# Two recurrent scans on one core: loops written out step by step, and four identity products in half-width tiles

## What is computed

```python
def _L1_conv_ref(feature, conv_w, conv_b, prelu_a):
    Wc = conv_w[:, :, 0, 4]
    def step(prev, x_i):
        y = jnp.einsum('oc,nch->noh', Wc, prev) + conv_b[None, :, None]
        y = jnp.where(y >= 0, y, prelu_a * y)
        cur = y + x_i
        return (cur, cur)
    x = jnp.moveaxis(feature, 3, 0)
    _, fwd_rest = jax.lax.scan(step, x[0], x[1:])
    fl = jnp.concatenate([x[0:1], fwd_rest], axis=0)
    _, bwd_rest = jax.lax.scan(step, fl[-1], fl[:-1], reverse=True)
...
x = x + _L0_conv_ref(_gn(x), ...)
x = x + _L1_conv_ref(_gn(x), L1_conv_conv_w, L1_conv_conv_b, L1_conv_prelu_a)
x = x + _L2_conv_ref(_gn(x), ...)
x = x + _L3_conv_ref(_gn(x), L3_conv_W, L3_conv_b)
```

## Time and profile before

| | |
|---|---|
| median of three runs | 253.15 us (253.0 to 253.29) |
| the profiled execution | 252.99 us |
| its span, first to last instruction | 251.2 us |
| busy: matmul, vector, scalar, POOL | 246.5, 168.1, 97.7, 87.7 us |
| scan 1, first to last matmul | 68.6 to 128.5 us of the span |
| scan 3, first to last matmul | 192.4 to 248.7 us |
| granted TensorE clock | full speed all through |

### The profile page before, as it was taken

One profiled execution on the slowest core, in us unless ns is written; L12 is line 12 of the kernel. 1 busy time (PEld: TensorE's weight loads), 2 busy tenths in 40 slices (PEclk: granted clock), 3 DMA queues, 4 the chain that ended last, 5 costly groups with the idle time before them and its releaser, 6 DMA issues.

```text
span 251.2 us, 11069 instructions
## 1 busy us (share of the span) xinstructions
PE 246.5 (98%) x4492; PEld 218.9 (87%) x4492; DVE 168.1 (67%) x655; ACT 97.7 (39%) x231; POOL 87.7 (35%) x138
## 2 busy tenths in 40 slices
PE   8999999999999999999999999999999999999995
PEld 2778787888699999999997887788887999999995
DVE  2789468377767777777788866684777555555453
ACT  2144855424954434443445467744267000000000
POOL 0208002035347665677633400000063532343432
PEclk9999999999999999999999999999999999999999
DMA  6999100000000000000000000000000000011212
GB/s 210 401 364 420 72 1 0 3 0 0 0 4 4 0 0 0 0 0 0 0 1 3 0 0 4 0 0 0 3 1 0 5 0 0 0 42 63 84 63 84
DMA packets 5200, 11.49 MB, mean 46 GB/s; under 512 B 832, under 2 KB 3264, under 8 KB 4672
## 3 DMA queue, kind: packets, MB, share of 16 engines
q1 hardware_dynamic: 4752, 10.73, 11.5%
q10 hardware_dynamic: 432, 0.56, 0.7%
HBM read 9.19 MB, written 2.10 MB: 45 GB/s over the span
## 4 chain that ended last, share of the span: by engine, by line
PE 94%; DVE 2%; DMA 2%; POOL 1%; issue 1%; DVEq 0%; POOLq 0%
PE banks L528 46%; PE banks L393 22%; PE banks L476 11%; PE banks L405 6%; PE banks L336 2%; PE banks L437 2%; DMA x<-in_x 2%; PE banks L459 1%; PE banks L499 1%; POOL rstd L1110 1%; DVE st L735 1%; PE banks L510 1%; PE banks L371 0%; PE banks L360 0%; PE banks L349 0%
## 5 line engine op out<-in xcount | busy, mean ns | idle before, releaser
L528 PE MATMUL banks<-state,wc 128*64 128x64 f32 x3712 | 110.4, 223 | 0.1
L528 PEld LDWEIGHTS banks<-state,wc 128*64 128x64 f32 x3712 | 110.0, 138 | 0.3 <-DVE state L979 0.2
L393 PE MATMUL banks<-xn,w 128*128 128x256 f32 x256 | 60.8, 385 | 0.0
L393 PEld LDWEIGHTS banks<-xn,w 128*128 128x128 f32 x256 | 46.9, 190 | 7.8 <-issue 2.3
L963 DVE SCALAR_TENSOR_TENSOR state<-banks,negb,inb 128x64 f32<-128x64 f32 x116 | 29.3, 281 | 24.2 <-PE banks L528 24.1
L1110 POOL TENSOR_TENSOR rstd<-gvar,mhalf 128x2 f32<-128x2 f32 (+3 forms) x13 | 15.8, 1221 | 78.5 <-DVE gvar L810 74.7
L969 DVE SCALAR_TENSOR_TENSOR sloped<-banks,par,share 128x64 f32<-128x64 f32 x120 | 30.9, 281 | 14.1 <-PE banks L528 12.5
L476 PE MATMUL banks<-probT,xT 128*128 128x256 f32 x128 | 28.9, 379 | 0.0
L476 PEld LDWEIGHTS banks<-probT,xT 128*128 128x128 f32 x128 | 24.3, 190 | 3.3
L671 ACT COPY banks<-inb 128x256 f32 (+1 forms) x28 | 10.6, 377 | 31.1 <-DVE state L979 28.1
L642 ACT ACTIVATE rel<-banks,par 128x256 f32<-128x256 f32 x32 | 13.4, 472 | 20.3 <-PE banks L393 20.3
(11 more groups left out here) (115 smaller groups left out, 239.2 us busy)
## 6 DMA issues: line engine op xcount, KB each, us to landing
w<-in_w SPq DMA_DIRECT2D x2, 1024.0 KB, 12.9
xT<-in_xT SPq DMA_DIRECT2D x4, 512.0 KB, 12.3
wc<-in_wc SPq DMA_DIRECT2D x2, 1024.0 KB, 17.9
result<-xh SPq DMA_DIRECT2D x15, 128.0 KB, 1.8
x<-in_x SPq DMA_DIRECT2D x3, 512.0 KB, 8.7
x<-in_x SPq DMA_DIRECT2D x1, 256.0 KB, 4.3
x<-in_x ACTq DMA_DIRECT2D x1, 256.0 KB, 4.4
w<-in_w ACTq DMA_DIRECT2D x1, 256.0 KB, 4.9
```

What stands on the lines that cost most here:

```text
L393: mm = nc.tensor.matmul(bank[2 + m // 2][:, m % 2 * POS:(m % 2 + 1) * POS], w3[l][:, k, m * P:(m + 1) * P], xn_s[:, k], start=(k == 0), st ...
L528: mm = nc.tensor.matmul(bank[K * h + m][c:c + TILE, 0:COLS], wc[l][:, k, m * P + c:m * P + c + TILE], inb[:, 0, k] if zeroth else state[:, ...
```

## The change

All loops over steps, on the matrix, scalar, vector and POOL engines, become Python loops, so each step is written out with constants for its counts and addresses; the loop of SyncE stays. And the identity products of step 0 of scan 1 are cut into two tiles of 64 columns, as all others of the scan.

```diff
@@ -507,8 +507,10 @@
                     if m == 0:
                         pe.wait_ge(s.inb, NC - K)
                         pe.wait_ge(s.early, 1)
-                    nc.tensor.matmul(bank[m][:, 0:COLS], ident[:], inb[:, 1, m], start=False, stop=True,
-                                     skip_group_check=True).then_inc(s.y[m], 1)
+                    for c in range(0, P, TILE):
+                        mm = nc.tensor.matmul(bank[m][c:c + TILE, 0:COLS], ident[:, c:c + TILE], inb[:, 1, m],
+                                              start=False, stop=True, skip_group_check=True)
+                    mm.then_inc(s.y[m], 1)
@@ -548,7 +550,7 @@
                 scan_step(1, 0, 0, False)
                 scan_step(1, 1, 1, True)
-                with pe.Fori(0, T - 2) as i:
+                for i in range(T - 2):
                     for h in range(2):
                         scan_step(1, i * 2 + 2 + h, h, True)
@@ -692,13 +694,13 @@
                 act.wait_ge(s.inb, NC)
-                with act.Fori(0, (T - 1 - EARLY) // 2) as i:
+                for i in range((T - 1 - EARLY) // 2):
                     for h in range(2):
                         step_inputs(i * 2 + EARLY - 1 + h, i * 2 + EARLY + h, h)
                 step_inputs(T - 2, T - 1, 0)
                 act.wait_ge(s.taken, T - 1)
                 step_inputs(T - 1, T - 2, 1)
-                with act.Fori(0, (T - 4) // 2) as i:
+                for i in range((T - 4) // 2):
                     last = i * -2 + (T - 3)
                     for h in range(2):
                         step_inputs(i * 2 + T + h, last + -h, h)
@@ -1010,7 +1012,7 @@
                 dve.wait_ge(s.inb, NC)
-                with dve.Fori(0, (T - 1 - EARLY) // 2) as i:
+                for i in range((T - 1 - EARLY) // 2):
                     for h in range(2):
                         step(i * 2 + EARLY - 1 + h, i * 2 + EARLY + h, h)
@@ -1018,7 +1020,7 @@
                 step(T - 1, T - 2, 1)
-                with dve.Fori(0, (T - 4) // 2) as i:
+                for i in range((T - 4) // 2):
                     last = i * -2 + (T - 3)
                     for h in range(2):
                         step(i * 2 + T + h, last + -h, h)
@@ -1176,7 +1178,7 @@
-                with pool.Fori(0, (T - 4) // 2) as i:
+                for i in range((T - 4) // 2):
                     for h in range(2):
                         keep_state(i * 2 + 3 + h, 1 - h)
@@ -1187,7 +1189,7 @@
                 add_state(T - 1, T - 1, 1)
-                with pool.Fori(0, (T - 2) // 2) as i:
+                for i in range((T - 2) // 2):
                     last = i * -2 + (T - 2)
                     for h in range(2):
                         if l == 1:
```

## The result

The changed kernel is **slower**: 256.44 us (256.01 to 257.35, six runs) against 253.20 for the kernel before on the same chip (252.91 to 253.29, six runs). The ratio is 1.0136, 95% interval 1.0126 to 1.0146: +3.2 us. The forecast was 255.1, range 253.3 to 256.0. The sign and the two handovers that make a step longer were right; a term put at nothing left the sum 1.3 us short.

A forecast was written before the change was run, and what follows sets the result against it. The prediction took scan 1 to be bound by a closed ring between vector and matrix engine, scan 3 by the matrix engine's pace. +1.37 + 1.7 - 0.09 - 0.21 - 0.75 = +2.0 us gave 255.1, range 253.3 to 256.0.

The forecast's parts named there:

- Vector's waits: Scan 1 on vector: the wait for products becomes separate, 24 steps at 0.057, +1.37 us.
- The matrix engine's handover: Scan 1: one place too few for two waits, so the state's becomes separate; 28 handovers at 0.06, +1.7 us.
- Stalls of the loops: Scan 1: late steps behind a branch go, -0.09 us, and the stall at the turn (step 13 to 15), -0.21.
- the ring: Scan 1's closed cycle of vector and matrix engine, 1.914 us a loop step; any longer handover costs once per step.
- Identity products: Step 0 of scan 1: narrow tiles let step 1 start sooner, -0.75 us, bounds 0.6 and 1.1.
- Scan 3: Runs at the matrix engine's own pace, so writing out its loops changes nothing: 0.
- Instruction blocks: Written-out code: 26 more matrix engine fetches cost 0; vector's extra blocks allowed 0 to 0.4 us.
- Rival (c): Instruction blocks arrive late on matrix engine or vector; a tenth of each fetch uncovered adds 3 us, 258.1; chance 0.07.
- (a): Waits of written-out steps keep their places in the engines' queues, only gains remain: -1.05, 252.1 us; chance 0.12.
- (b): Only one engine pays for separate waits: vector alone 253.5 us, matrix engine alone 253.8; chance 0.09.
- (d): The change does nothing, as loops and switches of width are hidden; chance 0.02.
- (e): Matrix engine's loops stall now on a fetch at each of 28 turns; written out, 32 us go, 223; chance 0.01.

The follow-up runs named there:

- e3: Kernel before with only the loops of scalar, vector and POOL written out, the matrix engine's loops and identity products kept: 254.47 us, ratio 1.0060.
- e5: Changed kernel with vector's waits exchanged, products of unit 0 asked for first and inputs second: 254.82 us, ratio 1.0075.
- e4: Changed kernel with the matrix engine's waits exchanged, state asked for first and seeded inputs second: 254.00 us, ratio 1.0042.
- e2: Kernel before with only the matrix engine's two loops written out: 255.41 us, ratio 1.0094.
- e6: Changed kernel with the waits of both the matrix engine and vector exchanged: 251.77 us, ratio 0.9951.
- e1: Kernel before with only the identity products cut to 64 columns, all loops kept: 252.29 us, ratio 0.9969.
- e8: Changed kernel with 3 of 6 wide filler products before scan 1 replaced by 16 narrow ones, shifting code by 26 instructions: 256.05 us, ratio 1.0112.
- e6 again: The kernel of e6, unchanged, run once more beside e9 and e10: 252.15 us, ratio 0.9960.
- e9: The kernel of e6 with the matrix engine's loop of scan 3 kept: 251.88 us, ratio 0.9956.
- e10: The kernel of e5 with both of the matrix engine's loops kept: 252.00 us, ratio 0.9950.

## Why the prediction was wrong, point by point

**Vector's waits, +0.057 a step: right.** Products to first state went from 0.680 to 0.736 us in e3, and back to 0.680 when the order was exchanged (e5).

**The matrix engine's handover, +0.06: right.** The load follows the state after 104 ns instead of 43, and e4 takes it back to 43. A step grew by 0.068 with it (e2), as the matmul behind the load came later still. Together 2.036 us a step where 2.03 was forecast. The reason given, "there is one place too few", held too. What it missed is that the order in the code decides which wait keeps the place: the first one does, and the last becomes separate. That the likeliest form was forecast right was owed to step 1's example.

**Stalls of the loops, -0.09 and -0.21: about right.** 0.55 us of excess over 28 x 1.912 went; some 0.24 of it was the separate waits of the four periods already in the written form (4 x 0.06), which leaves 0.31 for 0.30. It is a cover and no cure: with the ring back at 1.91 us (e6) the turn takes 2.09 again. At the turn scalar's copy still waited for POOL, against the earlier trace rows:

```profile
99.86 0.38 ACT L673 COPY banks<-inb 128x256 f32<-128x256 f32 x1 [1.93 <-POOL inb L1173]
```

but the state it fed no longer waited for it; what is long at that step now is vector's block.

**Identity products, -0.75: right.** 0.81 to the first matmul of step 1; 0.85 by e1's median.

**Scan 3, 0: right in this profile** (56.23 us), though in the profiled executions of e2 and e8 it took 0.5 and 1.2 us more, in pauses at block borders.

**Instruction blocks, "so I cost them at 0": this is the step that failed.** It was a cover taken over from the wrong place: the unbroken run of scan 3 showed a fetch beside a full queue, and the argument "a round lasts 3.7 us" asked only whether the block comes in time. It does: before each of scan 1's nine gaps the last packet had landed over 1.5 us earlier. But where the border lies within eight loads behind a wait that stands apart, the step is longer by 0.07 to 0.13 us all the same, and once where it lies two loads ahead of one: nine times, 0.93 us. For vector the range held "0 to 0.4 us" and the sum nothing; it is 0.57 (steps 14 and 28). Together 1.5 us. Of the same stretch of 28 steps the forecast had 1.37 + 1.7 - 0.09 - 0.21 = +2.77 and the trace has +4.40: 1.63 short, of which the blocks are 1.5 and the rest is mostly the matrix engine's handover, 0.068 where 0.06 was forecast. That the whole came out only 1.3 short is owed to the start, which gave back 0.06 more than forecast, and to chance in the stretches ahead of scan 1 and behind scan 3. Rival (c) had this mechanism, but priced as a late fetch at every block and given 0.07. The trace of before could have warned: vector's first pair of scan 1, written out and behind a separate wait, ran in this form:

```profile
70.55 0.68 DVE L969 SCALAR_TENSOR_TENSOR sloped<-banks,par,share 128x64 f32<-128x64 f32 x2 [0.73 <-PE banks L510]
```

0.68 us where its neighbours take 0.48. Its pause lies between vector's instructions 191 and 192, counted in the trace with the sequencer's, and the later two between 319 and 320 and between 447 and 448, one block of 128 further each.

The Trainium skill (Runtime: NRT & Kernel Launch, Instruction fetch mechanics) calls the cost of crossing a block's border mostly hidden. The traces agree in most places without a held separate wait ahead of the border (the changed kernel's scan 3 at 56.23 us; e4 and e6, 13 fetches each and no long step in scan 1 but vector's or the turn). They don't behind such a wait (+0.07 to 0.13 us on the matrix engine, +0.20 and 0.37 on vector), nor in three steps of e6 again, one of e2's scan 3 and five of e8's.

**The rivals.** (a), (b), (d) and (e) are out: both engines paid (e2, e3), the changed kernel is slower and not 30 us faster, and e9 and e10 show the loops costing nothing that writing them out would save. Of (c) the mechanism came true, though not as a late fetch, and at half of its price.

## What to carry to other kernels

Where an operation needs several semaphores, ask first for the one that comes last: it stays with the operation, and the ones that are long fulfilled stand apart and cost nothing that these traces show. In a closed ring between two engines this was worth 4.7 us of 256 in the written-out kernel, more than anything that writing out or looping did. And price a border of instruction blocks by where it falls, just behind a wait or far from one, not only by whether the fetch is in time.

## What the runs showed of the hardware that was not expected

- A block border costs time even with the block there (last packet landed 1.5 us or more before each gap): 0.07 to 0.13 us on the matrix engine (256 instructions a block) and 0.20 to 0.37 on vector (128), if it comes just behind a separate wait that has held the sequencer. 26 instructions' shift made the nine in scan 1 vanish (e8), and so did moving the wait (e4). What the sequencer does in that time no trace shows.
- Away from such a wait a border mostly costs nothing, but in some executions it does: 0.06 to 0.21 us in three steps of e6 again, 0.10 to 0.27 in five of e8's scan 3, 0.47 in one of e2's. All these gaps lie at the same place of the count by 256.
- With the matrix engine's loop of scan 3 written out, the runs of one kernel spread over 0.5 to 2.4 us (e2, e4, e5, e6, e8, the changed kernel), with it kept over 0.1 to 0.8 (e1, e3, e9, e10).
- A wide tile between narrow ones cost more than its own columns: 0.36 us for two matmuls of 128 columns, 0.12 for the four of 64, and the dozen unchanged matmuls between two of them went from 0.50 to 0.35 us (at 70.64 us in the chain of before, 70.34 after). Whether the change of width or the wide weight load is the reason wasn't tried.
